# Result rows of a mixture of experts in halves of lower and higher expert, and the last expert's fixed tile computed last

## The reference

```python
x = x + attn(layernorm(x))     # linear attention with a feature map, and a sliding window of 64, 16 heads of 8
x = x + ffn(layernorm(x))

# ffn: 8 experts of width 256, each token goes to 2 of them
gout = x @ Wgate + bgate
topv, topi = top_k(gout, 2)
topw = softmax(topv)
x1 = x @ W1[e] + b1[e];  x2 = x @ W2[e] + b2[e];  z = x1 * x2
g = z @ Wg[e] + bg[e]
o = g * sigmoid(g) * (z @ Wl[e] + bl[e])
y = o @ W3[e] + b3[e]
out = sum over the token's two experts of topw * y
```

## Time and profile before

| | |
|---|---|
| time, median of 3 runs | 394.18 us (391.79 to 398.92) |
| the profiled execution | 396.04 us, its span 394.2 us |
| mean granted TensorE clock | 0.978 |
| busy: PE, PEld | 357.2 us (91%), 302.9 us (77%) |
| busy: DVE, ACT, POOL | 253.2 us (64%), 213.1 us (54%), 219.2 us (56%) |
| moved by DMA | 50.23 MB, mean 127 GB/s |

### The profile page before, as it was taken

One profiled execution on the slowest core, in us unless ns is written; L12 is line 12 of the kernel. 1 busy time (PEld: TensorE's weight loads), 2 busy tenths in 40 slices (PEclk: granted clock), 3 DMA queues, 4 the chain that ended last, 5 costly groups with the idle time before them and its releaser, 6 DMA issues.

```text
span 394.2 us, 15938 instructions
## 1 busy us (share of the span) xinstructions
PE 357.2 (91%) x5708; PEld 302.9 (77%) x5710; DVE 253.2 (64%) x1002; ACT 213.1 (54%) x574; POOL 219.2 (56%) x368
## 2 busy tenths in 40 slices
PE   6799899799999999999999988899999999999910
PEld 2457688688888787778888853899999999999910
DVE  4787565488886888868887765455555555555415
ACT  0577567356676665655665620655555555555400
POOL 5374644456875766667675454124666666666510
PEclk9999999899999999999999999999999999999975
DMA  7747989576769988849551002223343333333028
GB/s 200 204 134 136 175 159 157 149 98 91 190 152 164 165 183 185 192 80 153 125 138 46 19 32 61 64 84 122 126 133 118 124 124 120 121 123 116 13 60 261
DMA packets 89024, 50.23 MB, mean 127 GB/s; under 512 B 57002, under 2 KB 82252, under 8 KB 88946
## 3 DMA queue, kind: packets, MB, share of 16 engines
q1 hardware_dynamic: 85378, 43.43, 47.9%
q0 software_dynamic: 2272, 4.46, 3.5%
q10 hardware_dynamic: 1296, 1.31, 1.0%
HBM read 29.52 MB, written 11.98 MB: 105 GB/s over the span
## 4 chain that ended last, share of the span: by engine, by line
PE 81%; DVE 5%; DMA 5%; issue 3%; SPq 2%; POOL 2%; ACT 1%; ACTq 0%; POOLq 0%; DVEq 0%
PE ps L773 8%; PE ps L779 8%; PE ps L663 7%; PE ps L610 5%; PE ps L756 4%; PE ps L659 4%; PE ps L702 4%; PE ps L709 4%; PE ps L745 4%; PE ps L748 4%; PE ps L622 4%; PE ps L629 3%; PE ps L685 3%; DMA ks<-results 2%; PE ps L589 2%
## 5 line engine op out<-in xcount | busy, mean ns | idle before, releaser
L1360 POOL TENSOR_SCALAR_AFFINE_SELECT amat<-amat 128x512 f32<-128x512 f32 x64 | 41.0, 641 | 63.1 <-ACT amat L845 62.4
L1394 POOL DMA_INDIRECT results<-qas,mrowid x39 | 38.2, 980 | 66.2 <-DVE qas L1248 66.2
L858 ACT ACTIVATE pmat<-ps 128x512 f32<-128x512 f32 x64 | 38.4, 600 | 51.5 <-PE ps L663 51.5
L1161 DVE TENSOR_REDUCE mrow<-ps 128x4 f32<-128x512 f32 x64 | 43.8, 685 | 30.9 <-PE ps L610 30.9
L1230 DVE SCALAR_TENSOR_TENSOR qas<-ps,bcol,qas 128x128 f32<-128x128 f32 x78 | 26.8, 350 | 36.2 <-PE ps L779 32.4
L900 ACT ACTIVATE qas<-ps,bcol 128x128 f32<-128x128 f32 x78 | 24.4, 364 | 39.6 <-PE ps L745 39.6
L1240 DVE SCALAR_TENSOR_TENSOR qas<-ps,bcol,qas 128x128 f32<-128x128 f32 x78 | 23.9, 346 | 26.6 <-ACT qas L900 26.5
L845 ACT ACTIVATE amat<-ps 128x512 f32<-128x512 f32 x64 | 38.5, 601 | 1.9 <-DVE xscale L949 1.4
L1321 POOL DMA_INDIRECT routed<-routed_row,slot x32 | 32.6, 1018 | 10.3 <-issue 5.7
L663 PE MATMUL ps<-minus_ident,mlow 128*128 128x128 bf16 x256 | 35.5, 219 | 0.5 <-issue 0.5
L663 PE MATMUL ps<-minus_ident,mrow 128*128 128x128 bf16 x256 | 35.9, 220 | 0.0
(11 more groups left out here) (183 smaller groups left out, 930.7 us busy)
## 6 DMA issues: line engine op xcount, KB each, us to landing
kv_tok<-w SPq DMA_DIRECT2D x31, 256.0 KB
qa_parts<-wgl SPq DMA_DIRECT2D x12, 256.0 KB, 3.2
ks<-k_parts SPq DMA_DIRECT2D x32, 96.0 KB
qas<-qa_parts SPq DMA_DIRECT2D x32, 96.0 KB
xin<-routed SPq DMA_DIRECT2D x39, 72.0 KB, 1.9
ks<-k_parts SPq DMA_DIRECT2D x32, 64.0 KB
qas<-qa_parts SPq DMA_DIRECT2D x32, 64.0 KB
w<-in_W SPq DMA_DIRECT2D x4, 512.0 KB
```

What stands on the lines that cost most here:

```text
L858: a_(pmat[:, u % 2].rearrange("p g t -> p (g t)"), ps[:, ST, :], ACT.Exp).then_inc(exp_done, 1)
L1161: v.tensor_reduce(mrow[:, b], ps[:, SQ, :].rearrange("p (a k) -> p a k", k=CH), AX.X, ALU.max).then_inc(max_done, 1)
L1360: q.affine_select(out=amat[:, u % 2], in_=amat[:, u % 2], compare_op=ALU.is_ge, fill=0.0, base=0, pattern=[[0, 4], [1, CH]], channel_multi ...
L1394: q.indirect_dma_start(results, bass.IndirectOffsetOnAxis(mrowid[:, m:m + 1], 0), yw[:, m, :], None, bounds_check=RESULTS - 1, oob_is_err= ...
```

## The change

The result rows are no longer numbered by choice but by expert. `topf[:, 0] > topf[:, 1]` is 1 where the best expert has the higher number; there the first choice's row number goes up by 2048 and the second's down by 2048. So the first half of `results` holds every token's lower-numbered expert, the second half the higher-numbered one, and expert 7's rows all lie in the second half. This takes three VectorE instructions for each row block: one comparison and two multiply-adds on 128x1 operands, with a wait on the comparison between them, in `weights_row` and in `places_and_row`.

The fixed tiles are now 0 to 6 (experts 0 to 6) and 38 (expert 7's first tile); 7 to 37 are dynamic. SP waits for the scatters of tiles 0 to 37 only, then loads the lower half; ACT waits for all 39, as before, then loads the upper half. VectorE adds the four groups of the lower half to x first, then the four of the upper half, each followed by its output write.

```diff
+DYN = E - 1
...
+        def fixed(j):
+            return j < DYN or j == NT - 1
+
+        def fixed_expert(j):
+            return min(j, E - 1)
...
-                if j < E:
-                    row = j * REGION
+                if fixed(j):
+                    row = fixed_expert(j) * REGION
                 else:
-                    row = sp.value_load(table[0:1, 1, j - E:j - E + 1], min_val=0, max_val=E * REGION)
+                    row = sp.value_load(table[0:1, 1, j - DYN:j - DYN + 1], min_val=0, max_val=E * REGION)
...
-            for j in range(4, E):
+            for j in range(4, DYN):
                 load_tile(j, j % 4)
             sp.wait_ge(table_ready, 1)
             sp.wait_ge(padded, 16 * (E + 1))
-            for j in range(E, NT):
+            for j in range(DYN, NT):
                 load_tile(j, j % 4)
 
             for k in range(4):
-                sp.wait_ge(y_out[k], 16 * ((NT - k + 3) // 4))
+                sp.wait_ge(y_out[k], 16 * ((NT - 1 - k + 3) // 4))
             for g in range(NG):
-                sp.dma_start(res[0][...], half_of_results(0)[...]).then_inc(res_in[g], 16)
+                sp.dma_start(res[0][...], half_of_results(0)[...]).then_inc(low_in[g], 16)
...
             def weights_row(r):
 
                 n, b = r + 1, r % 2
+                v.tensor_tensor(swap[:], topf[:, 0:1], topf[:, 1:2], ALU.is_gt).then_inc(r_swap, 1)
+                dve.wait_ge(r_swap, n)
+                for k in range(2):
+                    t = v.scalar_tensor_tensor(out=vals[:, r, k, 1:2], in0=swap[:], scalar=float(N * (1 - 2 * k)), in1=vals[:, r, k, 1:2],
+                                               op0=ALU.mult, op1=ALU.add)
+                t.then_inc(r_ids, 1)
                 dve.wait_ge(r_egap, n)
...
+                dve.wait_ge(r_ids, n)
                 v.tensor_tensor(parts2[:], ...)
...
             for g in range(NG):
-                at = slice(g * GC, (g + 1) * GC)
-                dve.wait_ge(res_in[g], 32)
-                v.tensor_tensor(res[0][:, at], res[0][:, at], res[1][:, at], ALU.add).then_inc(res_sum, 1)
+                dve.wait_ge(low_in[g], 16)
+                v.tensor_tensor(x_all[:, group_at[g]], x_all[:, group_at[g]], res[0][:, group_at[g]], ALU.add).then_inc(res_sum, 1)
+            for g in range(NG):
+                dve.wait_ge(res_in[g], 16)
                 dve.wait_ge(res_sum, g + 1)
-                v.tensor_tensor(x_all[:, at], x_all[:, at], res[0][:, at], ALU.add).then_inc(out_sum, 1)
+                v.tensor_tensor(x_all[:, group_at[g]], x_all[:, group_at[g]], res[1][:, group_at[g]], ALU.add).then_inc(out_sum, 1)
```

More of the change, by code:

```diff
@@ L200, in build @@
         wsum = sb("wsum", [CH, 1])
+        swap = sb("swap", [CH, 1])
         parts2 = sb("parts2", [CH, 2, 2, E])
@@ L265, in build @@
             sem(n) for n in ("xaffine", "xh_ready", "x1_ready", "st2_done", "mv2_ready", "ve2_ready", "rstd2_ready", "h2_ready"))
-        done = sem("done")
+        done, r_swap, r_ids = sem("done"), sem("r_swap"), sem("r_ids")
         settled = sem("settled")
@@ L281, in build @@
         res_in = [sem(f"res_in{g}") for g in range(NG)]
+        low_in = [sem(f"low_in{g}") for g in range(NG)]
         res_sum, out_sum = sem("res_sum"), sem("out_sum")
@@ L301, in folded @@
             return c % (T // CH) != T // CH - 1, c - c // (T // CH)
+        def fixed(j):
+            return j < DYN or j == NT - 1
+        def fixed_expert(j):
+            return min(j, E - 1)
         def run_steps(engine, step, places=()):
             def expert_of(t):
-                if t < E:
-                    return t
+                if fixed(t):
+                    return fixed_expert(t)
                 if t not in known:
-                    if t == E:
+                    if t == DYN:
                         engine.wait_ge(table_ready, 1)
-                    known[t] = engine.value_load(table[0:1, 0, t - E:t - E + 1], min_val=0, max_val=E - 1)
+                    known[t] = engine.value_load(table[0:1, 0, t - DYN:t - DYN + 1], min_val=0, max_val=E - 1)
                 return known[t]
@@ L451, in load_tile @@
                     sp.wait_ge(meta_copied, j - 3)
[L452 to L453 removed]
+                if fixed(j):
+                    row = fixed_expert(j) * REGION
                 else:
[L455 removed]
+                    row = sp.value_load(table[0:1, 1, j - DYN:j - DYN + 1], min_val=0, max_val=E * REGION)
                 sp.dma_start(xin[:, k, :], routed[bass.ds(row, CH), :]).then_inc(xin_ready[k], 16)
[L457 to L458 removed]
+                if not fixed(j):
+                    if j >= DYN + 4:
                         sp.wait_ge(x1w_ready, j - 3)
[L460 removed]
+                    e = sp.value_load(table[0:1, 0, j - DYN:j - DYN + 1], min_val=0, max_val=E - 1)
                     sp.dma_start(wb12[:, k, :], w12[:, bass.ds(e, 1), :].rearrange("p a f -> p (a f)")).then_inc(wb12_in[k], 16)
@@ L737, in step @@
                     q = (k + 1) % 2
-                    w = w12[:, j + 1, :] if j + 1 < E else wb12[:, (k + 1) % 4, :]
-                    if j + 1 >= E:
-                        pe.wait_ge(wb12_in[(k + 1) % 4], 16 * ((j + 1 - E) // 4 + 1))
+                    w = w12[:, fixed_expert(j + 1), :] if fixed(j + 1) else wb12[:, (k + 1) % 4, :]
+                    if not fixed(j + 1):
+                        pe.wait_ge(wb12_in[(k + 1) % 4], 16 * ((j + 1 - DYN) // 4 + 1))
                     pe.wait_ge(xT_copied, j + 2)
@@ L764, in step @@
                     q = k % 2
-                    w = wgl[:, j] if j < E else wbgl[:, q]
-                    if j >= E:
-                        pe.wait_ge(wbgl_ready, j - E + 1)
+                    w = wgl[:, fixed_expert(j)] if fixed(j) else wbgl[:, q]
+                    if not fixed(j):
+                        pe.wait_ge(wbgl_ready, j - DYN + 1)
                     pe.wait_ge(z_ready, 2 * (j + 1))
@@ L1385, in step @@
             def step(j, k, turn, expert):
-                if E <= j + 1 < NT:
-                    if j + 1 >= E + 2:
+                if 0 <= j + 1 < NT and not fixed(j + 1):
+                    if j + 1 >= DYN + 2:
                         pool.wait_ge(l_ready, 2 * j)
```

4 lines of the change are left out of this document (3 added, 1 removed).

## The result

The changed kernel took 402.83 us in the median of four runs (398.69 to 407.05), the kernel before, on the same chip, 394.33 (391.79 to 398.92). The run of 407.05 us fell into a slower state of the chip, and the ratios here leave such runs out. The ratio is 1.018, with a 95% interval of 1.011 to 1.0251: slower, on the other side of the forecast of 390.6. In a later measurement of ten runs the same kernel's ratio was 1.0089 (1.0036 to 1.0141). Both intervals lie above 1, so the loss is real; its size is less sure, somewhere between 0.4% and 2.5%.

What follows compares the result with a forecast made beforehand. TensorE was taken to bound the kernel (81% of the span), DMA only its end. End -4.2, router's tail +0.35 and attention +0.3 sum to -3.55 us; from the median 394.18 that gives 390.6, range 387.0 to 396.0.

Steps and rivals of the forecast that it cites:

- VectorE's charge in the attention stage: Attention chunks: three new operations push the next one back 0.35 us, up to 1.16 if held; 0.3 us charged in all.
- the last scatter beside the reads: End of the kernel: tile 38's scatter, now full and beside reads, takes 2.8 us and lands at 380.87.
- the end's gain: From the last weighting on: earlier lower reads and one add less behind the last landing gain 4.2 us, bounds 5.9 and 0.3.
- the room of 0.60 and 0.47 us: Attention chunk: slack before TensorE wants the row maximum (0.60) and the counts (0.47), so 0.35 us fits.
- rival (b): Attention stage: GpSimd holds the new operations to 1.16 us, counts 0.69 us late in 13 chunks, 9.0 us; 399.3; chance 0.08.
- The argument against (b): Attention stage: the tensor-tensor's median is 248 ns, and operations behind a held one start after GpSimd's instruction.
- the lower reads' start: End: SP waits for the last scatter but one, so lower reads start at 377.25 instead of 380.34, 3.09 us earlier.
- their rate: End: the lower half's 1.05 MB moves at 250 GB/s, between the 171 and 354 seen before.
- the tile order at no cost: Expert stage: tile 7 becomes dynamic and weight copies move one tile forward, hidden beside matmuls; nothing charged.
- The upper reads: End: issued by ACT from 381.03, 0.7 us later than before; 1.15 MB at 250 GB/s end at 386.5.
- The range: The forecast's own range, 388.6 to 394.5: end gain between 5.9 and 1.5 us, attention charge between 0 and 1.5.
- The router's tail: After attention: row block 13's three operations delay the chain by 0.35 us; blocks 14 and 15 cost nothing.

## Why the prediction was wrong

**The steps that failed** are two terms of the sum: VectorE's charge in the attention stage, and the last scatter beside the reads, which made the end's gain too large. They are of about the same size.

**VectorE's charge.** Of the span from 0.35 us a chunk ("if nothing is held up") to 1.16 the prediction took 0.35 for most chunks, since the old tensor-tensor's median is 248 ns, and charged 0.3 us in all for those that are held. Measured: the comparison took over 0.8 us in most chunks, and the row maximum was pushed back by 0.72 us. That is inside the span, but over the room of 0.60 and 0.47 us, so TensorE waited for the maximum and for the counts, which the prediction had named as the sign of its rival (b). An undisturbed chunk lost 0.55 us, and all chunks together 2.4 us by the profiles and some 4 by the times. Rival (b) had the mechanism, with a chance of 8%; its price of 9.0 us, 0.69 in each of 13 chunks, was too high, since not every comparison meets the mask and not every chunk passes the delay on.

The upper figure for one held operation, 0.50 us, was too low as well, because it came from the old tensor-tensor, which starts later in the block, when most of the mask is over. The new comparison takes the place directly behind the layer norm's line, and there GpSimd's mask of 0.64 us starts at almost the same instant. A mean or a maximum by line tells nothing of this; the timeline of the chunk, with both engines side by side, does. The operations that had that place before, a tensor-scalar and a reciprocal, have one tensor input each and passed untouched, though the mask started 0.06 us ahead of them as well (185.91 and 185.97).

The argument against (b), that "those behind it start after GpSimd's instruction and need not be" held, was half right: the multiply-adds and the old tensor-tensor were indeed free. But the delay moved the subtraction behind the maximum into the next mask, which took part of it back. With one input for the comparison the sum came out the same, so in this queue a hold saved at one place can return at the next.

The Trainium skill's rule (GPSIMD Engine Reference, Specifications), that VectorE's instructions with two SBUF inputs contend with GpSimd, is what these runs bear out: 832 ns with two inputs, 200 with one, in the same place beside the same mask. They also bound it: beside GpSimd's power on 128x1 operands (unit 3), or beside its scatters (tail), the same comparison took 146 to 154. I had the rule in the text and let the median row outweigh it.

**Right:** the lower reads' start (0.4 us after the last weighting, predicted 377.25 against 376.94), their rate (249 GB/s against 250), and the tile order at no cost (131.52 against 131.46).

**The last scatter: right in mechanism, wrong in size.** The prediction said that it "runs beside reads, so I take 2.8"; it took 4.67. So the upper reads were issued 389.90 - 383.96 = 5.94 us after the last weighting, where the forecast had 381.03 - 376.94 = 4.09 and the kernel before needed 3.40. These 1.85 us are most of what the end fell short by, 4.2 - 1.7 = 2.5. The other 0.6 stand behind the last landing, 4.05 us instead of 3.45: the four output writes were issued within 2.2 us instead of 4.8, and the last of them took 3.3 us to the end instead of 2.7. The upper reads themselves went as forecast, 5.5 us from issue to the last landing. The range took 1.5 us as the least gain of the end, where the prediction's own bound was 0.3; the measured 1.7 lies just inside.

**Not seen:** that adding the whole lower half first gives up the writes among the reads. It costs 2.3 us when both halves are read together; how much of it is left in the changed kernel, where the lower half comes first anyway, no run has separated. The router's tail lost 0.85 us instead of 0.35; 0.44 of it stays when block 13's operations are moved (17.87), so blocks 14 and 15 were probably not free; no run has them apart.

**Open:** why the one-input kernel in the old place, whose profile is repaired, was not measurably faster than the kernel before; why the first measurement's loss was twice the second's; and in which order the DMA engines serve the scatter's packets among the reads'.

## What to carry to other kernels

Before a small VectorE instruction is put into a steady loop, look at the timeline for what GpSimd runs at that very place. If the instruction has two SBUF tensor inputs and GpSimd works through a wide tile there, its price was here the rest of GpSimd's instruction, and of the copy that followed without a gap, and not its own 0.15 us. A form with a per-partition scalar, or another place in the loop, was free of that. A read that is started early gains less if something that the rest waits for lands behind it: here the scatter behind it came 2.6 us later and the end gained 1.7 us; with the read done before the last scatter was issued the end gained 4.0.

## What the runs showed of the hardware

- A 128x1 VectorE instruction with two SBUF inputs took 146 to 154 ns when GpSimd worked on no wide tile, and 819 to 879 when it started within 0.1 us after a GpSimd mask of 0.64 us (49 comparisons of six profiles). It then ended 15 to 28 ns after the end of the copy that followed the mask. Two more, of 584 and 714 ns, ended 7 and 45 ns after the mask itself. Beside the copy alone it took 242 to 253.
- The same work with one tensor input and a scalar read from SBUF took 199 to 218 ns, in either place, beside GpSimd or not.
- A scatter of one tile landed in 2.1 to 2.6 us with no reads of results beside it, and in 4.25 to 5.17 when four reads of 256 KB each began to be issued 0.2 to 0.9 us ahead of it on another queue. The landing came 0.1 to 0.3 us after that of one of these reads.
